# Three lines in GpSimd's prologue: a wait for the score of eight blocks back before blocks 8, 10, 12 and 14

## The chip, the cores and the metric

The kernel runs on one core of a Trainium2 chip. The metric is the device time of one execution in microseconds (us); the kernel before was timed in three runs. One further execution was taken by the hardware profiler, and all rows below come from that one. The engines are TensorE (PE), VectorE (DVE), ScalarE (ACT), GpSimd (POOL) and SyncE (SP), and 16 DMA engines move data for all of them.

## The reference, cut to what matters

A graph layer with 12,500 nodes of 64 features and 412,500 edges with 32 attributes each; the edges are sorted by destination.

```python
h = relu(layernorm(x))                                  # 12500 x 64
h0 = edge_attr @ W0 + b0                                # 412500 x 64
t = gelu(h0) @ W1 + b1
t = gelu(t) @ W2 + b2
score = (h0 + t) @ W3 + b3                              # 412500 x 64
msg = h[src] * score                                    # a gathered row per edge
wV = segment_sum(msg, dst) / max(count(dst), 1)         # 12500 x 64
out = x + wV @ Wo + bo
```

## The kernel before, in words

The edges are cut into 403 blocks of 1024, a block into 8 tiles of 128 edges. Every block takes the same road:

- SP loads the edge attributes twice, as `pair` (line 235) and as `act_in` (line 240, "attr" below), four blocks ahead, and a group of source indices `idx` per eight blocks (line 230). For the blocks after the first four, `pair` waits for `h0_done` and `act_in` for `score_done` (line 282) of the block four back.
- POOL issues 8 indirect DMAs per block (line 329). Each gathers 128 rows of 64 values of `h` into `rows`, which has 16 slots, one for a block (`G_RING = 16`).
- PE computes `h0` (line 431, `first`), `h1` (line 437, `second`) and the score (line 446, `last`, 8 tiles into `ps_sa` or `ps_sb`), and later adds the block's messages up by destination (line 455, `sums`, into `ps_wa` or `ps_wb`). Its order per block is: `second(b)`, `first(b+1)`, `sums(b-1)`, `last(b)`. Even blocks use the buffers that end in a, odd blocks those that end in b. Every one of these four steps ends in a semaphore increment by its last matmul: `h1_done`, `h0_done`, `sums_done`, `score_done`.
- ACT takes the two gelus (line 386, which waits for `h0_done`, and line 391, which waits for `h1_done`).
- DVE makes the one-hot matrix of the destinations (line 607), multiplies score and gathered rows (line 615, `message`: waits for `score_done` of the block and for its 8 gathers) and adds a finished window to `acc` (line 720).

Before the blocks can flow there is a prologue. `h` must be computed for all nodes and written to DRAM (`h_rows`) before anybody can gather from it. So POOL gathers the first 6 blocks (`RAW = 6`) from the raw `x`, and DVE and ACT normalise these rows in place. Blocks 6 to 15 are then gathered from `h_rows`, in a plain sequence of 80 indirect DMAs, with one wait ahead of block 8 (for the block bounds, because blocks 8 to 15 use space in `rows` that first held the destinations). From block 16 on POOL runs `gather_ahead` (line 345): for block b + 16 it waits for the message of block b, and, for even blocks, also for the score of block b + 8, that is of the block eight before the one it is about to gather (`LAG = 8`, line 350). So in the loop POOL works in bursts of two blocks, 16 gathers.

The change is in the prologue's loop at line 338. What consumes its gathers are the `message` steps of blocks 6 to 15 on DVE, behind the scores of PE, whose block loop (`steps`, line 499) starts with block 2.

Of the kernel before, what the change touches and what calls it, by code (L numbers as in the profile page):

```python
# [51 lines left out]
LAG = 8  # L52
# [22 lines left out]
def edge_gated_layer(nc, x, edges, src, dst, dst_rows, weights, out):  # L75

    with ExitStack() as ctx:
# [6 lines left out]
        def sem(name):  # L84
            return ctx.enter_context(nc.semaphore(name))
# [88 lines left out]
        score_done = sem("score_done")  # L174
# [29 lines left out]
        def blocks_loop(eng, first, end, unroll, step):  # L204

            turns = (end - first) // unroll
            if turns < 2:
                turns = 0
            else:
                with eng.Fori(0, turns) as i:  # L210
                    for u in range(unroll):
                        step(i * unroll + (first + u), first + u)
            for b in range(first + turns * unroll, end):
                step(b, b)

        def uses(b, ring):

            return (b >> ring.bit_length() - 1) + 1

        def tiles_of(b):  # L220
            return LAST_TILES if isinstance(b, int) and b == NB - 1 else TILES
# [95 lines left out]
        @block.gpsimd  # L317
        def _(pool):
            pool.iota(iota_i[:, :], pattern=[[1, WIN]], base=0, channel_multiplier=0
                      ).then_inc(set_up, 1)  # L320

            def gather(b, s, table):
                slot, part, at = s % G_RING, s // IDX_GROUP % IDX_GROUPS, s % IDX_GROUP
                if at == 0:
                    pool.wait_ge(idx_in[part], uses(b, IDX_GROUP * IDX_GROUPS) * 16)

                pool.sem_inc(gathers_begun, 1)
                for t in range(tiles_of(b)):
                    pool.indirect_dma_start(  # L329
                        rows[:, slot, t, :], None, table,  # L330
                        bass.IndirectOffsetOnAxis(ap=idx[:, part, at, t:t + 1], axis=0),
                    ).then_inc(gathered[slot], 16)

            for b in range(RAW):
                gather(b, b, x)

            pool.wait_ge(h_out, 32 * LN_STEPS)
            for b in range(RAW, G_RING):
                if b == G_RING // 2:

                    pool.wait_ge(bounds_step, 1 + 2 * CHUNKS)
                    pool.sem_inc(gathers_begun, 1)
                gather(b, b, h_dram)

            def gather_ahead(b, s):

                pool.wait_ge(msg_done, b + 1)
                if s % 2 == 0:

                    pool.wait_ge(score_done, b + (G_RING - LAG + 1))  # L350
                gather(b + G_RING, s + G_RING, h_dram)

            blocks_loop(pool, 0, NB - G_RING, IDX_GROUP * IDX_GROUPS, gather_ahead)
# [492 lines left out]
```

## Time and profile before

| | us |
|---|---|
| median of 3 runs | 4955.2 |
| lowest and highest run | 4943.95 and 4957.94 |
| the profiled execution's own time | 4910.35 |
| its span, first to last instruction | 4908.4 |

| engine | busy us | share of the span |
|---|---|---|
| PE | 3760.6 | 77% |
| PE weight load | 2533.1 | 52% |
| POOL | 3082.5 | 63% |
| ACT | 987.5 | 20% |
| DVE | 708.9 | 14% |

A timeline row gives the start in us, the duration, the engine, the line and the operation, and in brackets how long the engine was idle before it and what ended that: an engine with the instruction that released it, "issue" (the engine waited for nothing that the profile shows) or "remote" (it waited on a semaphore, and the profile matches no event to the release). TensorE's granted clock was 0.999 of full speed, and no slice of the span is below 0.9.

### The profile page before, as it was taken

What the parts mean: (1) busy time and instruction counts of PE and PEld (TensorE: products, weight loads), DVE (VectorE), ACT (ScalarE), POOL (GpSimd) and SP (SyncE); (2) the same over time, 40 slices, a digit from 0 to 9 for tenths busy, and PEclk for the clock granted to TensorE, in tenths of its full rate; (3) what the DMA queues carried; (4) which work ended last, traced back from release to release, by engine and by line L of the source; (5) the groups of instructions that cost most, each with busy time, mean ns of one, the idle gap of its engine ahead of it and who ended that gap; (6) DMA issues with size and microseconds to landing.
All of it is one profiled execution on the core that took longest, in us unless ns stands there. A gap on an engine that the chain in (4) does not pass through costs nothing.

```text
span 4908.4 us, 44284 instructions
## 1 busy us (share of the span) xinstructions
PE 3760.6 (77%) x14718; PEld 2533.1 (52%) x14719; DVE 708.9 (14%) x1349; ACT 987.5 (20%) x1332; POOL 3082.5 (63%) x3228
## 2 busy tenths in 40 slices
PE   2487777777777777777777777777777777777788
PEld 1355555555555555555555555555555555555566
DVE  5011111111111111111111111111111111111122
ACT  3112112221122211221122211222112121121211
POOL 7366666666666666666666666666666666666661
PEclk9999999999999999999999999999999999999999
DMA  4111111111111111111111111111111111111111
GB/s 122 28 46 44 45 44 46 46 45 44 44 46 46 44 45 44 46 47 44 44 45 45 46 44 44 44 45 47 44 44 46 44 47 44 44 46 44 46 37 47
DMA packets 223796, 227.46 MB, mean 46 GB/s; under 512 B 118540, under 2 KB 118669, under 8 KB 223352
## 3 DMA queue, kind: packets, MB, share of 16 engines
q0 software_dynamic: 103136, 105.82, 9.9%
q1 hardware_dynamic: 119968, 117.76, 8.4%
q10 hardware_dynamic: 616, 3.20, 0.2%
q14 instruction: 68, 0.56, 0.0%
q8 instruction: 8, 0.13, 0.0%
HBM read 220.11 MB, written 6.40 MB: 46 GB/s over the span
## 4 chain that ended last, share of the span: by engine, by line
another core or an unknown queue 63%; PE 25%; DVE 4%; DVEq 3%; issue 3%; POOL 1%; ACT 0%; DMA 0%; ACTq 0%; POOLq 0%
PE ps_sb L446 14%; PE ps_wa L455 8%; DVE msg L615 3%; DVEq L715 2%; POOL rows L329 1%; DVEq L614 1%; PE ps_sa L446 1%; PE ps_h1a L437 0%; PE ps_h0a L431 0%; PE ps_h0b L431 0%; PE ps_wb L455 0%; PE ps_h1a L484 0%; PE ps_h1b L437 0%; DVE acc L720 0%
## 5 line engine op out<-in xcount | busy, mean ns | idle before, releaser
L329 POOL DMA_INDIRECT rows<-h_rows,idx x3175 | 3026.5, 953 | 1739.0 <-issue 1005.5
L455 PE MATMUL ps_wa<-ln_sq,msg 128*65 128x64 f32 x3230 | 407.2, 319 | 1035.2 <-DVE msg L615 1035.2
L455 PEld LDWEIGHTS ps_wa<-ln_sq,msg 128*65 128x65 f32 x3230 | 369.7, 229 | 1348.6 <-DVE msg L615 1335.1
L391 ACT ACTIVATE act_in<-ps_h1b,wp 64x512 f32<-64x512 f32 x402 | 275.0, 684 | 2446.5 <-remote 2377.6
L446 PE MATMUL ps_sa<-w_last,act_in 97*128 97x64 f32 x3232 | 729.9, 420 | 11.1 <-ACT act_in L391 9.2
L446 PE MATMUL ps_sb<-w_last,act_in 97*128 97x64 f32 x3216 | 728.1, 421 | 0.6 <-ACT act_in L391 0.6
L446 PEld LDWEIGHTS ps_sa<-w_last,act_in 97*128 97x128 f32 x3232 | 711.9, 332 | 13.0 <-ACT act_in L391 9.0
L446 PEld LDWEIGHTS ps_sb<-w_last,act_in 97*128 97x128 f32 x3216 | 710.4, 333 | 2.3 <-issue 1.5
L615 DVE TENSOR_TENSOR msg<-ps_sa,rows 128x512 f32<-128x512 f32 x202 | 139.7, 691 | 3034.6 <-remote 2973.3
L391 ACT ACTIVATE act_in<-ps_h1a,wp 64x512 f32<-64x512 f32 x404 | 276.4, 684 | 1308.7 <-PE ps_h1a L437 1019.2
L455 PEld LDWEIGHTS ps_wb<-ln_sq,msg 128*65 128x65 f32 x3216 | 368.1, 229 | 303.5 <-issue 302.9
L437 PE MATMUL ps_h1b<-g,wp 128*128 128x512 f32 x402 | 406.4, 1112 | 35.7 <-ACT g L386 29.9
L431 PE MATMUL ps_h0a<-pair,wp 64*128 64x512 f32 x404 | 418.5, 1137 | 1.9 <-issue 1.9
L437 PE MATMUL ps_h1a<-g,wp 128*128 128x512 f32 x404 | 408.3, 1114 | 15.1 <-ACT g L386 13.4
L431 PE MATMUL ps_h0b<-pair,wp 64*128 64x512 f32 x402 | 416.5, 1138 | 0.0
L455 PE MATMUL ps_wb<-ln_sq,msg 128*65 128x64 f32 x3216 | 405.6, 319 | 1.5 <-issue 1.5
L615 DVE TENSOR_TENSOR msg<-ps_sb,rows 128x512 f32<-128x512 f32 x201 | 139.0, 692 | 985.9 <-PE ps_sb L446 905.8
L607 DVE TENSOR_TENSOR ln_sq<-dst_i,iota 128x512 f32<-128x512 f32 x403 | 277.8, 690 | 8.4 <-issue 8.4
L431 PEld LDWEIGHTS ps_h0a<-pair,wp 64*128 64x128 f32 x404 | 101.2, 309 | 304.3 <-issue 304.2
L431 PEld LDWEIGHTS ps_h0b<-pair,wp 64*128 64x128 f32 x402 | 100.3, 310 | 302.4 <-issue 302.4
L386 ACT ACTIVATE g<-ps_h0b,wp 128x512 f32<-128x512 f32 x201 | 138.2, 687 | 89.9 <-PE ps_h0b L431 51.5
L386 ACT ACTIVATE g<-ps_h0a,wp 128x512 f32<-128x512 f32 x202 | 138.9, 688 | 12.4 <-PE ps_h0a L431 5.5
(63 smaller groups left out, 719.4 us busy)
## 6 DMA issues: line engine op xcount, KB each, us to landing
pair<-in_edges SPq DMA_DIRECT2D x403, 128.0 KB
act_in<-in_edges SPq DMA_DIRECT2D x403, 128.0 KB
rows<-h_rows,idx POOLq DMA_INDIRECT x3175
xs<-in_x SPq DMA_DIRECT2D x4, 700.0 KB
h_rows<-ln_d ACTq DMA_DIRECT2D x4, 700.0 KB
dst_i<-in_dst SPq DMA_DIRECT2D x1, 1612.0 KB
idx<-in_src SPq DMA_DIRECT2D x50, 32.0 KB
rows<-in_dst_rows SPq DMA_DIRECT2D x4, 384.0 KB
```

The source lines that it names most:

```text
L329: pool.indirect_dma_start(rows[:, slot, t, :], None, table, bass.IndirectOffsetOnAxis(ap=idx[:, part, at, t:t + 1], axis=0),).then_inc(gat ...
L386: act.activation(g1[:, s % 2, :], ps_h0[s % 2][:, :], ACT.Gelu, bias=b0).then_inc(g1_done, 1)
L391: act.activation(act_in[0:D, s % IN_RING, g, :], ps_h1[s % 2][g * D:(g + 1) * D, :], ACT.Gelu, bias=wp[g * D:(g + 1) * D, C_B1:C_B1 + 1]). ...
L431: pe.matmul(ps_h0[s % 2][:, :], w0, pair[:, s % IN_RING, :], start=True, stop=True).then_inc(h0_done, 1)
L437: pe.matmul(ps_h1[s % 2][:, :], w1, g1[:, s % 2, :], start=True, stop=True).then_inc(h1_done, 1)
L446: mm = pe.matmul(ps_s[s % 2][:, t * D:(t + 1) * D], act_in[:, s % IN_RING, g, j * P:(j + 1) * P], w_last[:, :], start=(t == 0), stop=(t == ...
L455: last = pe.matmul(window, msg[:, s % 2, t, :], onehot[:, t, :], start=(t == 0), stop=(t == n - 1))
L607: return dve.tensor_tensor(to, rel.unsqueeze(2).to_broadcast([P, TILES, WIN]), iota_tiles, ALU.is_equal)
L614: dve.wait_ge(gathered[s % G_RING], (uses(b, G_RING) - 1) * 16 * TILES + 16 * n)
L615: dve.tensor_tensor(msg[:, s % 2, 0:n, 0:D], ps_s[s % 2][:, 0:n * D].rearrange("p (t d) -> p t d", d=D), rows[:, s % G_RING, 0:n, :], ALU. ...
L715: base = dve.value_load(base_b[0:1, one(b)], min_val=0, max_val=N - 1)
```

## The change

In the prologue's loop POOL gets one more wait ahead of blocks 8, 10, 12 and 14: for `score_done` to have reached 1, 3, 5 and 7, that is for the scores of blocks 0, 2, 4 and 6. Nothing else is touched; the number of gathers, their order and the slots are the same.

```diff
@@ -340,6 +340,9 @@
 
                     pool.wait_ge(bounds_step, 1 + 2 * CHUNKS)
                     pool.sem_inc(gathers_begun, 1)
+                if b >= LAG and b % 2 == 0:
+
+                    pool.wait_ge(score_done, b - LAG + 1)
                 gather(b, b, h_dram)
 
             def gather_ahead(b, s):
```

## Rows read from the trace of the kernel before

**Rows 1.** The page: the chain of work that ended last, by engine.

```profile
another core or an unknown queue 63%; PE 25%; DVE 4%; DVEq 3%; issue 3%; POOL 1%; ACT 0%; DMA 0%; ACTq 0%; POOLq 0%
```

**Rows 2.** Waits from 312 to 4800 us: total us, times, longest us.

```profile
DVE msg L615 <- remote: 2890.1, 193, 15.9
...
POOL rows L329 <- remote: 663.5, 176, 4.1
```

**Rows 3.** Busy time by stage: stretch, us, PE, PEld, DVE, ACT, POOL busy (count), PEclk, DMA, GB/s.

```profile
119.00:178.00 59.00, 0.74 (x1) 0.00 (x0) 0.00 (x0) 0.00 (x0) 44.67 (x48) 1.00 0.12 26
178.00:187.00 9.00, 0.00 (x0) 0.00 (x0) 0.00 (x0) 0.00 (x0) 0.67 (x1) 1.00 0.03 7
187.00:241.00 54.00, 52.09 (x213) 36.61 (x214) 9.40 (x19) 14.90 (x20) 0.00 (x0) 1.00 0.11 30
```

**Rows 4.** POOL's timeline, prologue: first gather of block 8, last of 9, first of 10, last of 15.

```profile
98.62 0.95 POOL L329 DMA_INDIRECT rows<-h_rows,idx  x1 [0.30 <-issue]
...
117.69 0.95 POOL L329 DMA_INDIRECT rows<-h_rows,idx  x1 [0.31 <-issue]
118.94 0.95 POOL L329 DMA_INDIRECT rows<-h_rows,idx  x1 [0.30 <-issue]
...
177.72 0.95 POOL L329 DMA_INDIRECT rows<-h_rows,idx  x1 [0.30 <-issue]
```

**Rows 5.** POOL's timeline: first of block 16, last of 17, of 19, of 21, first of 22.

```profile
241.45 0.95 POOL L329 DMA_INDIRECT rows<-h_rows,idx  x1 [62.78 <-PE ps_sa L446]
...
260.68 0.95 POOL L329 DMA_INDIRECT rows<-h_rows,idx  x1 [0.30 <-issue]
...
283.93 0.95 POOL L329 DMA_INDIRECT rows<-h_rows,idx  x1 [0.30 <-issue]
...
307.33 0.95 POOL L329 DMA_INDIRECT rows<-h_rows,idx  x1 [0.30 <-issue]
312.04 0.95 POOL L329 DMA_INDIRECT rows<-h_rows,idx  x1 [3.76 <-remote]
```

**Rows 6.** PE's timeline: the scores of block 2 and of block 14.

```profile
109.00 3.68 PE L446 MATMUL ps_sa<-w_last,act_in 97*128 97x64 f32 x16 [8.81 <-ACT act_in L391]
...
299.72 3.62 PE L446 MATMUL ps_sa<-w_last,act_in 97*128 97x64 f32 x16
```

**Rows 7.** DVE's timeline: the messages of blocks 2, 8, 12, 13 and 14.

```profile
187.54 0.69 DVE L615 TENSOR_TENSOR msg<-ps_sa,rows 128x512 f32<-128x512 f32 x1 [82.23 <-remote]
...
240.72 0.69 DVE L615 TENSOR_TENSOR msg<-ps_sa,rows 128x512 f32<-128x512 f32 x1 [7.43 <-PE ps_sa L446]
...
287.98 0.69 DVE L615 TENSOR_TENSOR msg<-ps_sa,rows 128x512 f32<-128x512 f32 x1 [13.93 <-remote]
...
294.37 0.69 DVE L615 TENSOR_TENSOR msg<-ps_sb,rows 128x512 f32<-128x512 f32 x1 [4.64 <-PE ps_sb L446]
...
311.46 0.69 DVE L615 TENSOR_TENSOR msg<-ps_sa,rows 128x512 f32<-128x512 f32 x1 [15.33 <-remote]
```

**Rows 8.** ACT's timeline: the second gelus of blocks 3 and 15.

```profile
189.49 1.40 ACT L391 ACTIVATE act_in<-ps_h1b,wp 64x512 f32<-64x512 f32 x2 [77.75 <-remote]
...
311.33 1.40 ACT L391 ACTIVATE act_in<-ps_h1b,wp 64x512 f32<-64x512 f32 x2 [12.63 <-remote]
```

**Rows 9.** SP's timeline: attr loads behind the scores of blocks 0, 2, 10, 12 and 14.

```profile
58.91 0.36 SPq L240 DMA_DIRECT2D act_in<-in_edges  x1
...
187.34 0.32 SPq L240 DMA_DIRECT2D act_in<-in_edges  x1
...
264.30 0.32 SPq L240 DMA_DIRECT2D act_in<-in_edges  x1
...
287.81 0.32 SPq L240 DMA_DIRECT2D act_in<-in_edges  x1
...
311.28 0.32 SPq L240 DMA_DIRECT2D act_in<-in_edges  x1
```

**Rows 10.** DMA queues from 118.64 to 178.67 us: packets, MB, share of 16 engines.

```profile
q0 software_dynamic: 1536, 1.58, 12.1%
```

## The prediction

> **What bounds the kernel now.** I read the chain of waits first. 63% of it ends in "another core or an unknown queue" [rows 1], so the end is set by waits that no recorded event explains, not by an engine's work. The list of waits names them: DVE's message waited so 193 times, 2890.1 us in all, and POOL's gather 176 times, 663.5 us [rows 2]. To see what such a wait hangs on I laid the engines' timelines beside each other, first in the loop.
>
> In one period of the loop POOL's burst of 16 gathers ends at 307.33 + 0.95 = 308.28 [rows 5]. PE's score of block 14 ended at 299.72 + 3.62 = 303.34 [rows 6], yet the three that wait for PE at that moment all go on much later and together: SP at 311.28 [rows 9], ACT at 311.33 [rows 8], DVE at 311.46 [rows 7]. POOL itself, which waits for the same score, issues again at 312.04 [rows 5]. Early in the burst nothing is late: the message of block 13 at 294.37 follows PE directly [rows 7]. So, as these rows have it, what PE signals late in a burst is not seen until POOL stops issuing. The attr load of SP dates the release: 264.30 - (260.68 + 0.95) = 2.67 us after the last gather, 287.81 - (283.93 + 0.95) = 2.93 and 311.28 - 308.28 = 3.00 [rows 5, 9]. Three out of three; why it is so the profile doesn't say.
>
> The prologue has the same picture once, and larger. POOL issues without a pause; blocks 10 to 15, 48 gathers, run from 118.94 to 177.72 + 0.95 = 178.67 [rows 3, 4]. PE's score of block 2 ended at 109.00 + 3.68 = 112.68 [rows 6]. SP sees it at 187.34, DVE at 187.54 after 82.23 us of waiting, and ACT runs block 3's second gelu at 189.49 after 77.75 us [rows 7 to 9]. From 119 to 178 us PE was busy 0.74 us, DVE and ACT not at all [rows 3]. The release is 187.34 - 178.67 = 8.67 us after POOL's last gather. Then, with all 16 slots full and POOL silent, PE runs blocks at its own pace: PE 52.09 busy of 54 us [rows 3], message 2 to message 8 in 240.72 - 187.54 = 53.18 us [rows 7]. Only the score of block 8 lets POOL go on, at 241.45 [rows 5].
>
> **The change part by part.**
>
> *The wait ahead of block 8* asks for the score of block 0. SP saw that one by 58.91 [rows 9], POOL comes to block 8 at 98.62 [rows 4]. Cost nothing beyond an instruction; the gap between gathers is 0.30 us with or without waits that are met [rows 4]. Blocks 8 and 9 are issued as before, until 117.69 + 0.95 = 118.64.
>
> *The wait ahead of block 10* asks for the score of block 2. PE raised it at 112.68, but nobody has seen it at 118.64. POOL therefore stops. Queued behind the wait are the 48 gathers of blocks 10 to 15, which DVE needs for messages 10 to 15 alone, eight and more blocks later. By the mechanism above, the stop is what releases the others. When? Nearest rows: 2.67 to 3.00 us after bursts of 16, 8.67 us after the long unbroken run [rows 4, 5, 9]. This run is 59 us shorter than that one but far longer than a burst, so I take the middle, 5.7 us: release at 124.3 (121.3 to 127.3). Message 2 follows 0.20 us behind SP, as before (187.54 - 187.34): 124.5 in place of 187.54, a head start of 63.0 us (60.0 to 66.0).
>
> *The waits ahead of 12 and 14* take part of it back. Blocks 10 to 15 now go out in three bursts, each let go by the score of eight blocks back, which is exactly the loop's rhythm. PE loses its undisturbed run over blocks 2 to 8. The loop's pace over three bursts is message 8 to message 14: 311.46 - 240.72 = 70.74 us [rows 7]; before, the same number of blocks took 53.18 us. Given back: 70.74 - 53.18 = 17.56 us. Message 8 comes at 124.5 + 70.74 = 195.3 and block 16 of the gathers starts 0.7 us later, in place of 240.72 and 241.45.
>
> Bounds of this term: below, if PE signals were never late in these three bursts, only POOL would pace them: 16 gathers at (177.72 - 118.94)/47 = 1.25 us are 20.0 us, plus 0.76 from release to first gather (312.04 - 311.28), so 62.4 us for three and 9.2 given back. Above, PE, DVE and ACT pass their loop bodies for the first time beside gathers; PE's early blocks have no row for that, and I allow another 10 us, 27.6 given back. I keep 17.6, which is measured on the same pattern.
>
> *Behind message 8* nothing changes: every later step waits on another engine, never on a time, so the whole rest moves up by the same amount. The message of block b is covered, since its gathers were issued eight scores earlier.
>
> Sum: 63.0 - 17.6 = 45.4 us saved. Ends: 60.0 - 27.6 = 32 and 66.0 - 9.2 = 57. Made against the profiled execution's 4910.35 us (4908.4 of span and 1.95 around it) it gives 4865. That execution is 44.9 us shorter than the median of the runs, 4955.2; where the rest of theirs goes I can't see, so I carry the difference over unchanged: 4955.2 - 45.4 = 4910.
>
> *A rule against it.* From 118.64 to 178.67 the gathers took 12.1% of the 16 DMA engines [rows 10]. The Trainium skill (DMA: Bandwidth & Descriptors, Queues, rings and completion order) says that each DMA engine goes round-robin between the queues that have work, packet by packet. By this rule the gathers of POOL can hold back no other queue, and a pause of POOL would buy nothing; the row agrees that there was no congestion. It leaves the release rows unexplained, and they decide for me; by the rule the time would be that of rival 2, 4973.
>
> **The rivals.**
>
> 1. *POOL sees the score of block 2 at once* (the lateness lies in how the others wait). Then it runs on through block 11, to 118.64 + 20 = 138.6, and stops ahead of block 12, whose score can't exist. Release at 141.6 to 147.3, messages 2 to 4 undisturbed (2 x 8.86 = 17.7 us at the pace of 53.18/6), then two bursts of 23.58: message 8 at about 144.7 + 17.7 + 47.2 = 209.6, saving 31 us: 4924. Against it: in the loop POOL needed until 312.04 for a score that ended at 303.34 [rows 5, 6].
>
> 2. *The release at 187.34 has nothing to do with POOL's stop* and comes when it comes. This is the slower side. POOL then stands idle ahead of block 10 from 118.64 to 187.34, and blocks 10 to 15 are gathered in bursts beside PE where before they were already there: all of the 17.56 us and no head start, 4955.2 + 17.6 = 4973. It decides from the point where message 2 comes later than 240.72 - 70.74 = 170.0 us. For it: the lag of 8.67 us, three times that of the bursts, and DMA queues that are nearly empty. Against it: three releases out of three behind a burst's end.
>
> 3. *The bursts of the prologue are slower than the loop's.* If the three took 35 us or more each in place of 23.6, the saving would be at most 63.0 - (105 - 53.2) = 11 us: no change that can be told, 4944 or more, say 4950. For it only that the engines pass new code there; against it, the first burst after the prologue (message 8 to 12 took 287.98 - 240.72 = 47.3 us for two bursts) was at the loop's pace at once [rows 7].
>
> That the change does nothing would need the score of block 2 to be seen before 118.64; SP's wait until 187.34 excludes it unless POOL alone sees it, which is rival 1.
>
> **How the numbers follow.** Forecast (4898 to 4923, from the ends 57 and 32): 76%. Rival 1: 8%. Rival 2: 8%. Rival 3: 8%. A measurement of this kernel tells about 0.3% (15 us) from no change. Faster by more than that: the forecast and rival 1, 84%; the same: rival 3, 8%; slower: rival 2, 8%. The runs spread over 14 us, so I widen the forecast's range by 6 us below and reach up into rival 3: 4892 to 4946. Likeliest: 4910.
>
> **What would show it.** In the changed kernel's trace: POOL idle behind 118.6 us for 3 to 9 us; SP's attr load and message 2 at 121 to 128 us instead of 187; three bursts of 16 gathers with gaps of 3.4 to 4 us; message 8 near 195 us, and block 16's first gather at once behind it without the gap of 62.78 us; after it a pace of 23.6 us for two blocks. POOL busy as before. I am wrong if POOL's gap ahead of block 10 is 60 us or more (rival 2), if it is absent and one stands ahead of block 12 (rival 1), or if message 8 comes after 225 us.

## The result and the profile after

| | median us | lowest to highest | runs |
|---|---|---|---|
| before | 4955.07 | 4943.95 to 4959.70 | 6 |
| changed | 4910.49 | 4900.28 to 4929.81 | 6 |

The ratio is 0.9923, with a 95% interval of 0.9900 to 0.9947: 44.6 us less, where 45.4 were forecast. The record doesn't name the chip on which these twelve runs were taken.

The profiled execution of the changed kernel took 4912.28 us (span 4910.3), no less than the profiled one of before (4910.35). These two can't be subtracted: they ran at different paces in the loop, which the change doesn't touch. The groups of instructions of POOL from 330 to 4600 us show it (count, busy, idle before), before first, changed second:

```profile
L329 POOL DMA_INDIRECT rows<-h_rows,idx x2898 | 2752.2, 950 | 1519.2 <-issue 878.9 <-remote 640.3
```

```profile
L329 POOL DMA_INDIRECT rows<-h_rows,idx x2875 | 2740.2, 953 | 1530.6 <-issue 874.2 <-remote 656.4
```

In the same 4270 us 23 gathers fewer, which is 23/16 bursts of 23.6 us, some 34 us. The profiled execution of before also lies outside its six timed runs (4910.35 against 4943.95 to 4959.70), while that of the changed kernel is one of its own six; so the two profiles were probably not taken under the same conditions. Later runs (below) show that the chip makes a far larger difference than the change. So I compare medians that were measured together, and traces mostly by their prologue.

The prologue of the changed kernel, POOL's timeline: the last gather of block 9, the first of 10, the last of 11, the first of 12, 14, 16 and 18.

```profile
119.30 0.95 POOL L329 DMA_INDIRECT rows<-h_rows,idx  x1 [0.30 <-issue]
121.56 0.95 POOL L329 DMA_INDIRECT rows<-h_rows,idx  x1 [1.31 <-remote]
...
140.31 0.95 POOL L329 DMA_INDIRECT rows<-h_rows,idx  x1 [0.30 <-issue]
153.41 0.95 POOL L329 DMA_INDIRECT rows<-h_rows,idx  x1 [12.16 <-PE ps_sa L449]
177.10 0.94 POOL L329 DMA_INDIRECT rows<-h_rows,idx  x1 [3.80 <-remote]
201.03 0.95 POOL L329 DMA_INDIRECT rows<-h_rows,idx  x1 [4.22 <-remote]
224.74 0.94 POOL L329 DMA_INDIRECT rows<-h_rows,idx  x1 [4.00 <-remote]
```

And DVE's timeline, the messages of blocks 2, 3, 4, 6 and 8:

```profile
121.00 0.69 DVE L618 TENSOR_TENSOR msg<-ps_sa,rows 128x512 f32<-128x512 f32 x1 [20.32 <-remote]
146.44 0.69 DVE L618 TENSOR_TENSOR msg<-ps_sb,rows 128x512 f32<-128x512 f32 x1 [23.65 <-remote]
152.84 0.69 DVE L618 TENSOR_TENSOR msg<-ps_sa,rows 128x512 f32<-128x512 f32 x1 [4.64 <-PE ps_sa L449]
...
176.53 0.69 DVE L618 TENSOR_TENSOR msg<-ps_sa,rows 128x512 f32<-128x512 f32 x1 [9.05 <-remote]
...
200.30 0.69 DVE L618 TENSOR_TENSOR msg<-ps_sa,rows 128x512 f32<-128x512 f32 x1 [10.59 <-remote]
```

Message 2 comes at 121.0 in place of 187.54 and message 8 at 200.3 in place of 240.72 [rows 7]; POOL's idle time of 62.78 us ahead of block 16 [rows 5] is gone. One thing doesn't fit. POOL's gap ahead of block 10 is 1.31 us and its last gather ended at 120.25; message 2 was there 0.75 us later, not 3 to 9. The gap that costs time is the one ahead of block 12, 12.16 us. It stands behind message 3, for which DVE waited 23.65 us, and that wait has two parts. PE itself was late with block 3: its score started behind ACT at 127.88 and ended at 132.29, 11.3 us behind message 2. PE stayed slow: over the four matmuls that follow, to 143.53, it stood idle for 1.1 to 2.5 us ahead of each, "issue". Then the finished score was held for 14 us, to SP's attr load at 146.26, 5.0 us behind POOL's last gather (141.26). PE's last rows of that score:

```profile
127.88 3.46 PE L449 MATMUL ps_sb<-w_last,act_in 97*128 97x64 f32 x15 [4.12 <-ACT act_in L394]
132.02 0.27 PE L449 MATMUL ps_sb<-w_last,act_in 97*128 97x64 f32 x1 [0.68 <-issue]
```

### The profile page after: what moved, and what is told of

Its sections match the earlier page's. It is cut to its first block, busy times and chain, and to the rows that moved or that the text cites. A ratio compares the mean times of both kernels' runs of the same rounds, so it can differ in the third digit from the quotient of the medians.

```text
span 4910.3 us, 44284 instructions
## 1 busy us (share of the span) xinstructions
PE 3765.9 (77%) x14718; PEld 2538.0 (52%) x14719; DVE 708.8 (14%) x1349; ACT 986.9 (20%) x1332; POOL 3095.2 (63%) x3228
## 4 chain that ended last, share of the span: by engine, by line
another core or an unknown queue 66%; PE 22%; DVE 4%; DVEq 4%; issue 3%; DMA 0%; ACT 0%; SPq 0%
PE ps_sb L449 12%; PE ps_wa L458 6%; DVE msg L618 3%; DVEq L718 2%; DVEq L617 1%; PE ps_sa L449 1%; PE ps_h0a L434 0%; PE ps_h1b L440 0%; PE ps_wb L458 0%; DVE acc L723 0%; PE ps_h1a L440 0%; PE ps_h0b L434 0%; PE ps_h1a L487 0%; PE ps_h1b L487 0%
```

## The experiments

"Held" below means: PE's score is done by the trace, and the engine that waits for it goes on several us later, "remote". DVE's idle time in the brackets is longer than the hold, because it starts before the score is done. The edits are shown against the changed kernel, and "..." stands for lines left out. The first four kernels ran on one chip, where the kernel before took 4904.18 us.

**Only the wait ahead of block 10.**

```diff
-                if b >= LAG and b % 2 == 0:
+                if b == 10:
```

> Only the wait ahead of block 10 is kept, those ahead of 8, 12 and 14 are left out. Theory (while POOL issues gathers, what PE signals is seen late or not at all; POOL's stop releases it): message 2 at about 121 us as in the changed kernel, then POOL issues 48 gathers without a break until about 182 and the other engines are held again after a block or two; they are released at 182 to 190, PE then runs undisturbed, message 8 at 224 to 233 us in place of 200 (changed kernel) and 241 (before). Time 8 to 17 us under the kernel before: 4938 to 4947. Rival (one stop is enough, what was held up was the engines' entry into their block loops): no second hold, message 8 at 174 to 192 us, 4888 to 4906.

Measured: 4899.51 us, ratio 0.9988 (0.9979 to 0.9997), 4.7 us under before. In its profile the score of block 2 was seen at once, so the wait was met and POOL issued without a stop to 180.57. This trace therefore doesn't show what the wait does when it isn't met. Messages 2, 3 and 4:

```profile
102.82 0.69 DVE L618 TENSOR_TENSOR msg<-ps_sa,rows 128x512 f32<-128x512 f32 x1 [5.53 <-PE ps_sa L449]
161.77 0.69 DVE L618 TENSOR_TENSOR msg<-ps_sb,rows 128x512 f32<-128x512 f32 x1 [57.16 <-remote]
191.39 0.69 DVE L618 TENSOR_TENSOR msg<-ps_sa,rows 128x512 f32<-128x512 f32 x1 [27.86 <-remote]
```

Two things follow. Held signals are not held until POOL stops: message 3 came through at 161.77 in the middle of POOL's run, 54 us after its score was done (107.49). And the second hold, which the rival excluded, is there. Against the 4904 us of before on this chip, the saving of 4.7 is less than either forecast (8 to 17, and 49 to 67); message 8 came at 225.3 us, where the theory had 224 to 233 and the rival 174 to 192.

**Only the waits ahead of blocks 12 and 14.**

```diff
-                if b >= LAG and b % 2 == 0:
+                if b in (12, 14):
```

> Only the waits ahead of blocks 12 and 14 are kept. Theory: POOL issues without a break to about 141 us and stops ahead of block 12, since no score of block 4 can exist; the release of message 2 comes with that stop, at 141 to 147 us, 20 us later than in the changed kernel; then bursts of two blocks. Message 8 at 205 to 212 us, 4919 to 4930. Rival (the release does not hang on POOL's stop, but comes at its own time): message 2 near 187 us as before, POOL idle until then, 4955 or more.

Measured: 4872.16 us, ratio 0.9937 (0.9924 to 0.9950), 32 us under before. Messages 2 and 3, then POOL's last gather of block 11 and first of block 12:

```profile
118.25 0.69 DVE L618 TENSOR_TENSOR msg<-ps_sa,rows 128x512 f32<-128x512 f32 x1 [18.78 <-remote]
145.05 0.69 DVE L618 TENSOR_TENSOR msg<-ps_sb,rows 128x512 f32<-128x512 f32 x1 [25.01 <-remote]
```

```profile
138.03 0.94 POOL L329 DMA_INDIRECT rows<-h_rows,idx  x1 [0.30 <-issue]
152.02 0.94 POOL L329 DMA_INDIRECT rows<-h_rows,idx  x1 [13.05 <-PE ps_sa L449]
```

The saving is what I expected (25 to 36 us under before), its course is not: message 2 came by itself while POOL issued, and what POOL's stop at 138.97 released, some 6 us later, is message 3.

**A pause in place of the waits.**

```diff
-                if b >= LAG and b % 2 == 0:
+                if b in (10, 12, 14):
 
-                    pool.wait_ge(score_done, b - LAG + 1)
+                    for k in range(4):
+                        pool.memset(pause[:, :], 0.0).then_inc(paused, 1)
+                        pool.wait_ge(paused, (b - 10) * 2 + k + 1)
```

> The waits are left out; ahead of blocks 10, 12 and 14 POOL instead writes zeros four times into a buffer of its own (128 x 1024, one after the other), so it is busy with something that is no gather for some 4 us and waits for no other engine. Theory (it is the issuing of gathers that holds PE's signals, and any stop of some us releases them): message 2 at 121 to 126 us, three bursts with these pauses between them, message 8 at 195 to 205 us, 4905 to 4925. Rival (only a POOL that waits for PE lets the others go, or 4 us are too short): engines held as in the kernel before until POOL is through with block 15, then near 190 to 200 us, message 8 near 250, 4960 to 4970.

(The buffer and the semaphore that this needs are added too and not shown.) Measured: 4862.88 us, ratio 0.9915 (0.9900 to 0.9929), 41.3 us under before. POOL's pauses, and SP's attr loads behind the scores of blocks 3, 5 and 7:

```profile
120.60 3.99 POOL L348 MEMSET pause<- 128x1024 f32 x4
...
145.42 3.99 POOL L348 MEMSET pause<- 128x1024 f32 x4
...
169.86 4.00 POOL L348 MEMSET pause<- 128x1024 f32 x4
```

```profile
123.78 0.32 SPq L242 DMA_DIRECT2D act_in<-in_edges  x1
...
148.10 0.32 SPq L242 DMA_DIRECT2D act_in<-in_edges  x1
...
172.84 0.32 SPq L242 DMA_DIRECT2D act_in<-in_edges  x1
```

Releases 3.2, 2.7 and 3.0 us behind the last gather, three of three, with POOL busy writing zeros. Message 2 was never held (105.50, where I expected 121 to 126), and message 8 came at 179.41, earlier than the 195 to 205 expected. Against the kernel before on the same chip (below) that is a lead of 54 us, and at message 14 it was down to 31: no pause stands ahead of block 16, so POOL ran through blocks 14 to 17, 32 gathers in a row, and message 9 came at 220.10, 31 us after its score was done (188.38). POOL's last gather of that run and SP's attr load, 5.5 us behind its end:

```profile
213.48 0.94 POOL L331 DMA_INDIRECT rows<-h_rows,idx  x1 [0.30 <-issue]
```

```profile
219.92 0.32 SPq L242 DMA_DIRECT2D act_in<-in_edges  x1
```

Stops with no wait for PE release, and a run without a stop holds again. So it is POOL's issuing of gathers that holds, not POOL at work and not the lack of a wait; the change's semaphore is only a way to make it stop at the right moment.

**The kernel before once more.**

> The kernel before once more, unchanged, with a profile. All theories: its time is that of the kernel before (4945 to 4960). Open question: the profiled execution of before took 4910 us at a granted clock of 0.999, the changed kernel's executions 4900 to 4930 at 0.511. If the clock goes with the 45 us, this profile shows a clock near 0.51, about 4955 us, and a loop period of two blocks near 23.73 us in place of 23.5.

Measured: 4903.37 us, ratio 0.9997 (0.9989 to 1.0006). Its profile took 4904.83 us at a granted clock of 0.512. The executions of before on this chip took 4896 to 4916 us and are listed at 0.51 or at 1.00 without order: so the clock column doesn't go with the 45 us, and that guess falls. Messages 2, 3 and 8 and POOL's last gather of block 15:

```profile
117.73 0.69 DVE L615 TENSOR_TENSOR msg<-ps_sa,rows 128x512 f32<-128x512 f32 x1 [20.19 <-remote]
190.56 0.69 DVE L615 TENSOR_TENSOR msg<-ps_sb,rows 128x512 f32<-128x512 f32 x1 [71.03 <-remote]
...
233.67 0.69 DVE L615 TENSOR_TENSOR msg<-ps_sa,rows 128x512 f32<-128x512 f32 x1 [7.43 <-PE ps_sa L446]
```

```profile
178.62 0.94 POOL L329 DMA_INDIRECT rows<-h_rows,idx  x1 [0.30 <-issue]
```

The same kernel as in [rows 7], and here it is message 3, not 2, that meets the long hold: its score was done at 130.38 and message 3 came 60 us later, 11.0 us behind the end of POOL's last gather (message 2 was held for 16 us, from 101.28). Which block meets the long hold varies from run to run; that one meets it was so in each of the three traces in which POOL issued blocks 10 to 15 without a stop (this one, [rows 7], and the kernel with the wait ahead of 10 alone).

**Four kernels on a second chip.** The kernel before took 4215.58 us there. The four are the changed kernel once more and these three edits of it: LAG 6, a wait ahead of every block, and plain copies in place of the gathers. The copies fetch 128 fixed rows and not the rows that the indices name, so that kernel doesn't compute the reference.

```diff
-LAG = 8
+LAG = 6
```

```diff
-                if b >= LAG and b % 2 == 0:
+                if b >= LAG:
...
-                if s % 2 == 0:
+                if True:
```

```diff
-                    pool.indirect_dma_start(
-                        rows[:, slot, t, :], None, table,
-                        bass.IndirectOffsetOnAxis(ap=idx[:, part, at, t:t + 1], axis=0),
-                    ).then_inc(gathered[slot], 16)
+                    pool.dma_start(
+                        rows[:, slot, t, :], table[t * P:(t + 1) * P, :],
+                    ).then_inc(gathered[slot], 16)
```

> The changed kernel once more, to be compared with the others on one chip (the kernel before took 4904 us on the last one, 4955 on the first). All theories: 0.990 to 0.995 of the kernel before, as measured first; some 40 us under it. Read beside the kernel that keeps only the waits ahead of 12 and 14 (32 us under the kernel before), it says what the wait ahead of block 10 is worth: 5 to 15 us if it releases message 2 in those executions in which that one is held for long, nothing if message 2 always comes through near 118 us by itself.

> LAG is 6 in place of 8, in the prologue (so the waits stand ahead of blocks 6, 8, ..., 14, for the scores of 0, 2, ..., 8) and in the loop. Theory (a stop of POOL's gathers lets PE's signals through; then one rhythm of some 23.6 us for two blocks up to PE's last 6 blocks, which take 9.2 us each): POOL's first stop is ahead of block 8, near 100 us instead of 120, message 2 at 103 to 107 us, so the rhythm begins 14 to 18 us earlier; at the end 2 blocks more go at 11.8 in place of 9.2 us, 5 us back. 8 to 13 us under the changed kernel. Rival (the lead of eight blocks is needed, because PE would wait for rows): 20 us or more over the changed kernel.

> POOL waits for the score of eight blocks back ahead of every block from 8 on, not of every second one, in the prologue and in the loop: bursts of 8 gathers (10 us) in place of 16 (20 us). Theory, two forms. If a stop always costs the 3.8 us that POOL idles between bursts now, a block takes 13.8 in place of 11.8 us: 800 us slower. If PE's signals are held only late in a burst (in the traces those up to about 8 us behind a burst's start were on time), the release is never waited for and a block takes 10.3 to 11 us: 300 to 600 us faster. I lean to the second, 60 to 40.

> Every gather is replaced by a plain copy of 128 fixed, adjacent rows, issued by POOL in the same place with the same bytes and semaphores, so the messages are made from the wrong rows; the rest is the changed kernel. If what holds PE's signals is POOL's making of descriptors for an indirect DMA (it reads 128 indices for each), holds and the 23.6 us rhythm go, the pace is PE's 9.2 us for a block, some 3800 us in all. If any DMA issued by POOL does it, the holds stay, with bursts that may be shorter: 4000 to 4900 us, and POOL's first gather of a burst still comes some 3 us or more behind the last of the burst before.

Measured: the changed kernel 4215.97 (ratio 1.0001, 0.9992 to 1.0010), LAG 6 4218.62 (1.0007, 0.9998 to 1.0016), a wait ahead of every block 4215.65 (1.0001, 0.9992 to 1.0010), plain copies 3820 and 2127 in two executions. All expectations for the first three were wrong, for one reason. The changed kernel's chain of waits by engine, and its longest wait from 90 to 4200 us:

```profile
POOL 73%; issue 23%; PE 3%; POOLq 1%; DVE 0%; DMA 0%; DVEq 0%
```

```profile
DVE msg L618 <- DMA rows<-h_rows,idx: 3235.0, 380, 9.1
```

Not one wait is "remote". From 90 us on POOL issues with no gap at any of the new waits or the loop's, and sets the pace with 10.3 us a block. The traces of the other two have no "remote" wait either. Nothing is held on this chip, and so the change is worth nothing.

**Four kernels on a third chip**, where the kernel before took 4904.18 us again.

> The changed kernel again. On one chip the kernel before took 4216 us and nothing was held: POOL issued without a stop, none of its waits was ever late, and the change was worth nothing. Theory: the worth of the change hangs on whether PE's signals are held while POOL issues, which differs between chips. Where the kernel before takes about 4900 us or more, the changed one is 35 to 48 us under it; where it takes about 4216 us, within 2 us of it.

> Only the waits ahead of 12 and 14, beside the whole change on one chip. If the wait ahead of block 10 releases message 2 (the prediction's step), this one is 5 to 20 us slower than the changed kernel. If message 2 comes through by itself near 118 us, as in this kernel's first profile, the two are within 4 us. On a chip without holds: both equal.

> Waits ahead of every block. On a chip with holds: 300 to 600 us faster than the kernel before if a burst of 10 us is over before a hold begins (the first late signal stood 8 to 15 us behind a burst's start), 800 us slower if each stop costs 3.8 us. On a chip without holds: equal, as before.

> Plain copies by POOL in place of the gathers (the messages are made from wrong rows). On a chip with holds: if it is the indirect DMAs that hold PE's signals, the pace is PE's, 3820 us, as on the chip without holds (3820 in its profiled run, at the slow matmul pace); if any DMA of POOL does it, 4000 us or more, with waits of other engines on something that no event explains.

| | median us | ratio | interval |
|---|---|---|---|
| changed | 4868.20 | 0.9921 | 0.9907 to 0.9934 |
| waits ahead of 12 and 14 only | 4878.37 | 0.9936 | 0.9923 to 0.9950 |
| a wait ahead of every block | 4858.49 | 0.9901 | 0.9886 to 0.9916 |
| plain copies | 3818 and 2127 | | |

The change is worth 36.0 us here, without the waits ahead of 8 and 10 25.8; the single executions of the two overlap (4862.15 to 4872.08 and 4867.93 to 4879.80). The two profiles show a way in which they can differ by 10 us: messages 2 and 3, of the whole change first, of the waits ahead of 12 and 14 second.

```profile
112.92 0.69 DVE L618 TENSOR_TENSOR msg<-ps_sa,rows 128x512 f32<-128x512 f32 x1 [14.60 <-remote]
145.30 0.69 DVE L618 TENSOR_TENSOR msg<-ps_sb,rows 128x512 f32<-128x512 f32 x1 [30.59 <-remote]
```

```profile
144.95 0.69 DVE L618 TENSOR_TENSOR msg<-ps_sa,rows 128x512 f32<-128x512 f32 x1 [47.41 <-remote]
151.34 0.69 DVE L618 TENSOR_TENSOR msg<-ps_sb,rows 128x512 f32<-128x512 f32 x1 [4.60 <-PE ps_sb L449]
```

With no wait ahead of block 10, a message 2 that is held stays so until the stop ahead of block 12. With the whole change message 2 came by itself, its wait was met, and message 3 was held to the stop ahead of 12 instead. The kernel with a wait ahead of every block can stop ahead of 11 too, which might close that hole; its one trace on this chip stopped ahead of 10 and not of 11, so that is not shown. Its POOL (first gather of block 10, then of 12) and its messages 2, 3 and 4:

```profile
123.39 0.94 POOL L329 DMA_INDIRECT rows<-h_rows,idx  x1 [4.38 <-remote]
146.86 0.94 POOL L329 DMA_INDIRECT rows<-h_rows,idx  x1 [3.81 <-remote]
```

```profile
122.83 0.69 DVE L618 TENSOR_TENSOR msg<-ps_sa,rows 128x512 f32<-128x512 f32 x1 [14.63 <-remote]
129.22 0.69 DVE L618 TENSOR_TENSOR msg<-ps_sb,rows 128x512 f32<-128x512 f32 x1 [4.59 <-PE ps_sb L449]
146.29 0.69 DVE L618 TENSOR_TENSOR msg<-ps_sa,rows 128x512 f32<-128x512 f32 x1 [15.31 <-remote]
```

This is the one trace in which the wait ahead of block 10 does what the prediction said: POOL stops at 119.0, message 2, whose score was done at 115.58, follows 3.8 us later, and the loop's rhythm of 23.5 us starts at once. My 300 to 600 us for this kernel were wrong, and the 800 us slower too: in the loop the score for the odd block is always there in time, so the bursts stay at 16 gathers. It has the best ratio of the versions that compute the whole result, 45.7 us under before here (its interval overlaps those of the change and of the pause), and it is equal to before on the chip without holds.

Plain copies give no "remote" wait on either chip. In the second profile, from 100 to 2050 us, POOL waits for PE, 1.5 us at most:

```profile
POOL rows L329 <- PE ps_sa L448: 184.6, 171, 1.5
```

So on the chip with holds too, POOL's direct DMAs of the same size don't hold PE's signals; its indirect ones do. They are also shorter to issue (16 copies in 8.4 us, against 20.0), so most bursts of them are over at about the time at which holds began in the other traces. The second profile has one longer run, 32 copies without a stop from 270.73 to 287.74, and a score that was done 12.6 us into it, at 283.34, was seen at once:

```profile
271.44 16.30 POOL L329 DMA_DIRECT2D rows<-h_rows  x31 [0.18 <-issue]
```

```profile
283.55 0.69 DVE L617 TENSOR_TENSOR msg<-ps_sb,rows 128x512 f32<-128x512 f32 x1 [3.09 <-PE ps_sb L448]
```

In the loop of the kernel before, a score done 14.8 us into a burst was held (burst from 288.56, score done at 303.34). One such run speaks against burst length as the reason, but doesn't settle it.

## Why the prediction was right, point by point

The direction and the mechanism that it rests on, breaks in POOL's gathers let PE's signals through, were right wherever the kernel before took 4904 us or more. That the number came within 0.8 us is luck: the step to which it gave the head start mostly did not happen as described, two misses offset each other, and the same change was worth 36.0 us on one other chip and nothing on another.

- *What bounds the kernel.* Right where it was read: POOL's gathers hold PE's signals, shown by the pause (releases 2.7 to 3.2 us behind the last gather, without any wait for PE) on the chips that have holds. But "not seen until POOL stops" was too strong. Held messages came through at 161.77 (message 3) and at 112.9 to 118.25 (message 2) while POOL issued on, and in two traces message 2 wasn't held at all (102.82 and 105.50).
- *The wait ahead of block 8.* No cost, as said: no gap ahead of it in any trace.
- *The wait ahead of block 10.* Predicted: POOL stops for 3 to 9 us, and that releases message 2 at 121.3 to 127.3. Message 2 came at 121.0 and the head start was 66.5 us in place of 63.0, but not through this wait: POOL stopped for 1.31 us, SP saw the score 0.55 us behind the last gather's end (120.80 against 120.25), where releases by a stop came 2.7 us or more behind it, and with the wait left out message 2 came at 118.25 in one profile and at 144.95 in another. By the signs that I had named, POOL's gaps (1.31 us ahead of 10, 12.16 ahead of 12) are nearer to rival 1 than to the forecast. What the waits ahead of 8 and 10 are worth is 4868.2 against 4878.4 us, some 10 us. The waits ahead of 12 and 14 alone gave the bulk of the gain, 25.8 to 32 us, and I had said of them that they only give back; the wait ahead of 10 alone gave 4.7.
- *Given back.* 17.6 us predicted from 70.74 us for three bursts. Messages 2 to 8 took 200.30 - 121.00 = 79.3 us, so 26.1 were given back, inside the bound of 27.6. The first pair took 152.84 - 121.00 = 31.8 us, the others 23.7 and 23.8: in the first, PE's own gaps in block 3 and the hold behind them. The bound had allowed for this, the 17.6 had not. The two misses offset each other: 66.5 - 26.1 = 40.4 us at message 8, against 45.4.
- *Behind message 8* everything moves up. On two chips of equal pace (2897 and 2898 gathers from 330 to 4600 us) message 8 stands at 233.67 before and 198.99 changed, 34.7 us, and the spans are 4902.8 and 4870.0, 32.8 us.
- *Rivals 1 and 3.* Rival 1 (POOL sees the score of block 2 at once and stops only ahead of 12) did happen, in the changed kernel's profile on the third chip, and with messages 2 and 3 at 112.9 and 145.3 its message 8 (198.99) comes as early as in the first profile (200.30), with 36.0 us saved in the median of that chip; rival 1 had said 31. I gave it 8%. Rival 3 is there in one slow burst of three.
- *Rival 2*, the slower side, is refuted by the pause. Nor were the signals held until the gathers' transfers were through: of the 8.67 us between POOL's last gather and the release, the last 7 (180.0 to 187.3 us) have no packet in any DMA queue. The time that I had tied to the round-robin rule, 4973, did not come. The Trainium skill's round-robin rule (DMA: Bandwidth & Descriptors, Queues, rings and completion order) is not contradicted by that, since the signals of PE's matmuls were what was held and not a DMA queue; I had drawn more from the rule than it says.
- *What no rival had*: that on another chip nothing is held and the change is worth 0.0 us (ratio 1.0001). The prediction carried one profile to all executions, and was lucky in the chip. The 44.9 us by which that profile was shorter than the timed runs were a sign of this; the prediction noted them and carried them over unchanged.

Why a chip holds or not stays open. So does why a release comes some 3 us behind a burst of 16 gathers in the loop, but 5 to 6.4 behind block 11, 5.5 behind the 32 gathers of the pause kernel and 8.7 to 10.8 behind an unbroken run to block 15, what lets some signals through while POOL issues on, and what the "issue" gaps of PE in the first block behind a hold are. Nothing recorded names the path on which PE's increments wait.

## What to carry to other kernels

When several engines that wait for one producer all go on together, just behind the end of another engine's burst, suspect the burst: break it at the point where its consumers are still covered, and try a bare pause first, which shows whether it is the stop or the wait that helps. Put such a stop ahead of every unit that may meet a hold, not only every second one (the wait ahead of every block had the best ratio, though not clear of the others); a wait that is met costs nothing that could be measured (4215.65 against 4215.58 us). And measure before and after on the same chip: the same kernel took 4216 or 4904 us on different ones and 4955 in the first measurement, far more than the change is worth.

## What the runs showed of the hardware that was not expected

- One program, three levels: 4215.58 us on one chip, 4904.18 on two, and 4955.07 in the first measurement, every timed execution within 0.3% of its median. The profiled execution of the kernel before, 4910.35 us, is 0.9% under its own six; whether it ran elsewhere is not on record. The kernel before was not profiled on the fastest chip; the four traces taken there have no held signal at all.
- The granted clock of the records doesn't give PE's pace. Eight tiles of a score take 3.62 us at a record of 1.00 (which would be the 2.4 GHz level) as at 0.50 (1.2 GHz). In the kernel with plain copies they took 3.62 us in the execution of 3818 us (record 0.999) and 1.95 us in that of 2124.5 us (record 0.965). Only the matmuls' durations tell the two apart.
